# A sorted mixture of experts: third payloads kept by GpSimd at the join, the next first comparison moved between the join's halves, exponentials and joint-point moves reordered

## The reference, cut to what matters

```python
for i in range(E):                                          # 16 experts
    gate_feature = hidden_states * pe[i] @ gate_w + gate_b  # 768 per token
    gate_weight, gate_idx = jax.lax.top_k(gate_feature, K)  # K = 384
    gate_weight = jax.nn.softmax(gate_weight, axis=-1)
    gathered = jnp.take_along_axis(hidden_states, gate_idx, axis=-1)
    y = y + _moe_mlp(gathered * gate_weight, eg_w[i], eu_w[i], ed_w[i])
```

## Time and profile before

| | us |
|---|---|
| median of 3 runs | 6527.94 (6523.31 to 6537.23) |
| profiled execution, its own time | 6528.06 |
| its span in the trace | 6526.2 |
| busy: TensorE, VectorE, ScalarE, GpSimd | 5668.0, 5168.4, 2656.1, 4136.3 |

### The profile page before, as it was taken

One profiled execution on the slowest core, in us unless ns is written; L12 is line 12 of the kernel. 1 busy time (PEld: TensorE's weight loads), 2 busy tenths in 40 slices (PEclk: granted clock), 3 DMA queues, 4 the chain that ended last, 5 costly groups with the idle time before them and its releaser, 6 DMA issues. The chain is left out here.

```text
span 6526.2 us, 70284 instructions
## 1 busy us (share of the span) xinstructions
PE 5668.0 (87%) x16428; PEld 2994.9 (46%) x16428; DVE 5168.4 (79%) x6614; ACT 2656.1 (41%) x4418; POOL 4136.3 (63%) x3675
## 2 busy tenths in 40 slices
PE   8989999889888888888888888888888888889988
PEld 4545554445444444444444444444444444445555
DVE  4011012999999999999999999999999999998841
ACT  0000001445454545454545454555555544544431
POOL 0543034668777777777777777777777776767740
PEclk9999999989999999999999999999999999999999
DMA  3365245000000000000000000000000000001101
GB/s 124 111 158 158 105 143 154 1 22 15 15 15 16 15 16 15 30 1 30 1 30 1 30 14 17 15 16 15 16 16 15 16 15 16 15 30 37 37 25 43
DMA packets 113770, 254.57 MB, mean 39 GB/s; under 512 B 36105, under 2 KB 46863, under 8 KB 113323
## 3 DMA queue, kind: packets, MB, share of 16 engines
q1 hardware_dynamic: 70442, 180.18, 7.9%
q0 software_dynamic: 42880, 69.46, 4.3%
HBM read 214.75 MB, written 34.58 MB: 38 GB/s over the span
## 5 line engine op out<-in xcount | busy, mean ns | idle before, releaser
L1370 PE MATMUL mask_ps<-key,neg_ident 125*125 125x480 f32 (+7 forms) x4128 | 1877.5, 573 | 583.2 <-DVE key L1757 576.9
L1465 POOL TENSOR_TENSOR pay<-pay_side,pay 125x480 int32<-125x480 int32 (+9 forms) x1120 | 1306.7, 1167 | 641.4 <-DVE pay L1780 633.2
L1643 ACT COPY mask_ps<-key 125x960 f32<-125x960 f32 (+7 forms) x1152 | 954.7, 829 | 1706.1 <-DVE pay L1797 1029.0
L1457 POOL TENSOR_TENSOR pay_side<-pay 125x480 int32<-125x480 int32 (+9 forms) x1120 | 1301.2, 1162 | 338.3 <-DVE pay L1797 160.9
L1370 PEld LDWEIGHTS mask_ps<-key,neg_ident 125*125 125x125 f32 x4128 | 729.1, 191 | 1473.6 <-DVE key L1757 1012.8
L1780 DVE COPY_PREDICATED pay<-mask_ps,pay 125x960 f32<-125x960 int32 (+6 forms) x1120 | 1240.4, 1108 | 58.5 <-POOL pay_side L1457 24.0
L1747 DVE TENSOR_TENSOR key<-mask_ps,key 125x960 f32<-125x960 f32 (+6 forms) x1120 | 1091.9, 975 | 61.7 <-PE mask_ps L1370 37.6
L1757 DVE TENSOR_TENSOR key<-mask_ps,key 125x960 f32<-125x960 f32 (+6 forms) x1120 | 1092.7, 976 | 0.0
L1370 PE MATMUL mask_ps<-key_top,neg_ident 125*125 125x480 f32 (+3 forms) x1472 | 607.1, 541 | 139.8 <-DVE key_top L1757 129.3
L1317 PE MATMUL slot_ps<-w_exp,hid 128*125 128x384 f32 x1920 | 672.4, 488 | 8.8 <-issue 8.8
L1289 PE MATMUL slot_ps<-u_feat,w_exp 128*128 128x312 f32 (+1 forms) x2304 | 666.2, 426 | 0.4 <-ACT u_feat L1533 0.4
(11 more groups left out here) (189 smaller groups left out, 5435.9 us busy)
## 6 DMA issues: line engine op xcount, KB each, us to landing
w_rel_g<-L_gnn_W SPq DMA_DIRECT2D x16, 2304.0 KB, 23.4
w_exp<-L_ffn_ed_w SPq DMA_DIRECT2D x16, 2304.0 KB, 8.4
messages_dram<-rows_g SPq DMA_DIRECT2D x12, 1875.0 KB
w_exp<-L_ffn_eg_w SPq DMA_DIRECT2D x16, 1152.0 KB, 5.5
w_exp<-L_ffn_eu_w SPq DMA_DIRECT2D x16, 1152.0 KB, 7.9
messages_dram<-rows_g SPq DMA_DIRECT2D x20, 375.0 KB
root_w_g<-L_gnn_root SPq DMA_DIRECT2D x2, 2304.0 KB
w_exp<-L_ffn_sg_w SPq DMA_DIRECT2D x4, 1152.0 KB, 5.7
```

The source lines that it names most:

```text
L1370: last = pe.matmul(mask, neg_ident[0:TP, 0:TP], operand, start=False, stop=True, skip_group_check=True)
L1457: pool.tensor_tensor(shares(pay_was(turn, u), turn, u)[1].bitcast(I32), first, second, ALU.add).then_inc(pays_added, 1)
L1465: pool.tensor_tensor(second, shares(pay_was(turn, u), turn, u)[1].bitcast(I32), first, ALU.subtract).then_inc(pays_taken, 1)
L1643: act.copy(seed_of(turn, u), compared(turn, u)[0]).then_inc(seeded, 1)
```

## The change

`keep_pays` goes from ScalarE to GpSimd, and from the second half of the join to the first: GpSimd does it at unit 91, after its last shares of units 89 and 90. Keys and payloads kept get a semaphore each. ScalarE seeds the next turn's unit 0 at unit 91, ahead of the payload copies of 91. `preset(2)` moves from unit 0 to unit 1, behind the seed of unit 2. VectorE compares the next turn's unit 0 between the keys of unit 92 and the payloads of 91, not behind the payloads of 91. At joint points VectorE does the second payloads of u-2 ahead of the larger keys of u, not behind. The exponentials go to units 40, 41, 42, 44 and 45, those of 39 to 46 in which ScalarE takes no gate result; the weighing is two units behind each (42, 43, 44, 46, 47), `invert` goes from 46 to 47, the scaling from 47..51 to 48..52, and `BEGIN` stays 52. The early products are spread over units 0 to 51, so that the first part of the first one is in unit 1, not 2, and those behind it in part one unit earlier. The set of free units changes with these, with as many shared columns in it as before (47450).

```diff
-        NSET, NKEPT = 3, 3
+        NSET, NKEPT = 3, 2
...
-        WEIGH = EXPS + 2
-        INVERT = EXPS + NT + 2
+        INVERT = EXPS + NT + 3
         SCALE = INVERT + 1
-        BEGIN = SCALE + NT
+        BEGIN = SCALE + NT - 1
...
-            todo = beside(turn, ahead, lag, 1, BEGIN)
+            todo = beside(turn, ahead, lag, 0, BEGIN)
...
-        REGULAR.free = {u for u in range(REGULAR.n) if not WEIGH <= u < WEIGH + NT
+        gates_taken = {spot - 1 for spot in asking}
+        exps_at = [u for u in range(EXPS, INVERT) if u not in gates_taken][0:NT]
+        weigh_at = [u + 2 for u in exps_at]
+        assert exps_at[NT - 1] < INVERT and weigh_at[0] < SCALE
+        REGULAR.free = {u for u in range(REGULAR.n) if u not in weigh_at
                         and all(work is nothing for work, _ in asking.get(u, []))}
...
+            def keep_pays(turn, i, u):
+
+                pool.wait_ge(pays_done, turn.done("units", i, u))
+                pool.wait_ge(pays_taken, turn.done("sums", i, u))
+                settle(pool, pool_waits)
+                pays = pay[:, :].rearrange("p (i b t) -> p i b t", b=BLK, t=NT)[:, :, 2, :]
+                for half in range(2):
+                    pool.tensor_copy(third_pays[half], pays[:, half * 128:half * 128 + 128, :]).then_inc(kept_pays, 1)
...
-                    if turn is REGULAR and WEIGH <= u < WEIGH + NT:
-                        if u == WEIGH:
+                    if turn is REGULAR and u in weigh_at:
+                        if u == weigh_at[0]:
                             features_sorted(turn, i, SORTED + 1)
-                        weigh(i - 1, u - WEIGH)
+                        weigh(i - 1, weigh_at.index(u))
                     for work, args in todo.get(u, []):
                         work(*args)
+                    if turn.units[u] == (JOIN, 0, 2):
+                        keep_pays(turn, i, u)
...
                     if u + 1 < turn.n:
                         seed(turn, i, u + 1)
-                    elif following is not None:
-                        seed(following, i + 1, 0)
                     if turn is not CLOSING and u == 0:
                         if turn is REGULAR:
-                            act.wait_ge(kept, i * NKEPT)
+                            act.wait_ge(kept_pays, i * NKEPT)
                         preset(0)
                         if turn is REGULAR:
                             act.wait_ge(pays_done, turn.done("units", i, 0))
-                        for q in range(1, NSET):
-                            preset(q)
+                        preset(1)
+                    if turn is not CLOSING and u == 1:
+                        preset(2)
                     if turn.units[u] == (JOIN, 0, 2):
                         keep_keys()
+                        seed(following, i + 1, 0)
                     copy_pays(turn, i, u)
-                    if turn is REGULAR and EXPS <= u < EXPS + NT:
-                        if u == EXPS:
+                    if turn is REGULAR and u in exps_at:
+                        if u == exps_at[0]:
                             keys_sorted(turn, i, i - 1, SORTED + 1)
-                        exponentials(i - 1, u - EXPS)
+                        exponentials(i - 1, exps_at.index(u))
...
-                    if turn.units[u] == (JOIN, 1, 2):
-                        keep_pays()
                     do(todo.get(u, []))
...
                     if turn is REGULAR and u == INVERT:
                         invert(i - 1)
+                    if u in turn.joint:
+                        second_pays(turn, i, u - 2)
                     larger_keys(turn, i, u)
-                    if u > 1:
+                    if u > 1 and u not in turn.joint:
                         second_pays(turn, i, u - 2)
                     smaller_keys(turn, i, u)
...
                 for u in range(max(turn.streams, 1), turn.n):
                     larger_keys(turn, i, u)
                     smaller_keys(turn, i, u)
+                    if turn.units[u] == (JOIN, 1, 2):
+                        larger_keys(following, i + 1, 0)
+                        smaller_keys(following, i + 1, 0)
                     first_pays(turn, i, u - 1)
                     second_pays(turn, i, u - 1)
-                if following is not None:
-                    larger_keys(following, i + 1, 0)
-                    smaller_keys(following, i + 1, 0)
```

More of the change, by code:

```diff
@@ L1064, in experts @@
                                                     sem("mask_made"))
-        kept, bias_set, bias_ready, slots_primed = sem("kept"), sem("bias_set"), sem("bias_ready"), sem("slots_primed")
+        bias_set, bias_ready, slots_primed = sem("bias_set"), sem("bias_ready"), sem("slots_primed")
+        kept_keys, kept_pays = sem("kept_keys"), sem("kept_pays")
         pay_copied, moved, pays_done, pay_set = sem("pay_copied"), sem("moved"), sem("pays_done"), sem("pay_set")
         pays_added, pays_taken = sem("pays_added"), sem("pays_taken")
-        sort_waits = sem("sort_waits")
+        sort_waits, pool_waits = sem("sort_waits"), sem("pool_waits")
         max_ready, exp_ready, inv_ready = sem("max_ready"), sem("exp_ready"), sem("inv_ready")
@@ L1618, in keep_keys @@
             def keep_keys():
-                act.copy(third_key, key[:, :].rearrange("p (i b t) -> p i b t", b=BLK, t=NT)[:, :, 2, :]).then_inc(kept, 1)
-            def keep_pays():
-                pays = pay[:, :].rearrange("p (i b t) -> p i b t", b=BLK, t=NT)[:, :, 2, :]
-                for half in range(2):
-                    act.copy(third_pays[half], pays[:, half * 128:half * 128 + 128, :]).then_inc(kept, 1)
+                act.copy(third_key, key[:, :].rearrange("p (i b t) -> p i b t", b=BLK, t=NT)[:, :, 2, :]).then_inc(kept_keys, 1)
             def preset(q):
@@ L1745, in larger_keys @@
                 if s == FLIP or (s == 0 and turn is not OPENING):
-                    dve.wait_ge(kept, (i - 1) * NKEPT + 1)
+                    dve.wait_ge(kept_keys, i)
                 dve.tensor_tensor(results(turn, u)[0], seed_of(turn, u), compared(turn, u)[1],
@@ L1771, in first_pays @@
                     dve.wait_ge(pays_taken, turn.done("sums", i, turn.needs[u]))
-                    dve.wait_ge(kept, i * NKEPT)
+                    dve.wait_ge(kept_pays, i * NKEPT)
                     settle(dve, sort_waits)
```

## The result

The changed kernel takes 6494.22 us (median of 4 runs, 6481.10 to 6502.65), a ratio to the kernel before of 0.9943 (95% interval 0.9932 to 0.9955): 34 us faster, where 58 were forecast. It is inside the range and nearest to the price of rival A, but not for A's reason. The profiled execution took 6502.65 us, 25.4 less than that of before, though its graph layer, which the change doesn't touch, took 7.5 more.

The account below looks back on a forecast made before the run. VectorE was taken to bound turns 2 to 14. Exponentials 20, joint points 7, join 25 and TensorE's clock 6 gave 58 us off 6528.06: 6470 us, with 6452 to 6502 for 8 in 10.

Parts of the forecast that it names:

- rival A: TensorE's clock and the order of its early products bring an 18 us loss, not the gain: 6494 us; chance 0.08.
- Bound: VectorE bounds turns 2 to 14; only its idle time, at most 10.55 us a turn, can be won.
- Exponentials: VectorE's waits for ScalarE's seeds at units 44 and 45 go: 1.45 us a turn, 20 us in all.
- Joint points: At units 75 and 81 VectorE's second payloads move into its wait for the mask: 0.5 us a turn, 7 us.
- Join: Around unit 92, VectorE's wait for ScalarE's `pay_top` copy goes and unit 0 starts earlier: 1.65 us each, 25 us in all.
- Rival D: GpSimd's copies at the join are slow and `preset(0)` waits; over 8.9 us for both the change loses; chance 0.03.
- the payload copy that the forecast set against it: VectorE's 640-column payload copy took 0.89 us beside GpSimd's `xs` scaling and 0.88 with GpSimd idle.
- Mask of unit 2: Behind the join, an earlier half product fills TensorE's idle time before this mask: 0.5 us a turn, 6 us.

Follow-up runs that it names:

- e7: The changed kernel with the two copies of the third payloads on ScalarE again, all else as changed: 6500.49 us, ratio 0.9962 to the kernel before.
- e5: The kernel before with only the order of moves at the joint points changed: 6526.3 us, ratio 0.9994 to the kernel before.
- e12: The changed kernel with early products and free units as before, but TensorE does the first product's first half in unit 1, not 2: 6482.85 us, ratio 0.9929.
- e2: The changed kernel with its free units computed from the old spread of early products: 6481.5 us, ratio 0.9929 to the kernel before; run again 6484.78 us, 0.9926.
- e1: The changed kernel with early products spread from unit 1 as before, so also the old column shares in the first 37 units: 6484.86 us, ratio 0.9941.
- e10: The changed kernel with the old free units, plus an unused half product on TensorE behind the masks of units 6, 76 and 84: 6478.49 us, ratio 0.9925.

## Why the prediction was right in its direction and short in its size

**Bound.** Right: VectorE's idle time was what could be won, and 7 us of 10 are still there.

**Exponentials** (forecast 1.45 us a turn). The seed waits went from 1.59 to 0.28, and from the larger keys of unit 43 to those of 50 a turn has 23.3 us in place of 25.0. Right.

**Joint points** (0.5). 0.4 at the place. Right, and too small to be seen alone.

**Join** (1.65). 1.3 to 1.7, 1.68 in the turn shown, with the residual wait of 0.46 on the preset named beforehand. Right. GpSimd's copies took 0.79 and 0.80 us, which is the lower bound, not the 2.5 us for both that I took. Rival D falls, and e7 shows that the copies needn't have moved. VectorE's comparisons beside them took 1.16 us each (2026.94), as in e7, where GpSimd stood idle. The lock of which the Trainium skill's page "SBUF — State Buffer", section "Who interferes with whom", tells needs two SBUF inputs for a `tensor_tensor` on VectorE; these comparisons have one (the seed lies in PSUM), so their agreement says nothing against it. Nor does the payload copy that the forecast set against it: its mask lies in PSUM, and beside that it takes one input from SBUF.

**Mask of unit 2** (0.5). 0.63 to 0.66 in 12 turns and 0.47 in one. The idle time ahead of this mask fell from 3.12 to 1.80 us; it takes 1.88 us in 8 of 13 turns and 2.3 to 3.0 in the others, and VectorE waits for it in one turn only, 0.09 us. Right in its size; that TensorE would work nearly without a break was not so, and e5 shows that this wait goes in some turns without the early product. The 18 us of rival A didn't come. The new wait before L1782 did (0.49 a turn), and e12 shows that some 0.3 of it count.

**The step that failed** is a sentence: "VectorE's and GpSimd's shares stay, since the free units hold the same number of columns". They do hold the same number (47450), but I counted the columns of the free units and not what freeing does in each. In units with two rows it does nothing, so VectorE's columns rose from 28835 to 29555 a turn. It costs 1.0 us a turn, 13 us, and e2 shows it by undoing it: its shortest turns take 313.2 us, and "about 313" was forecast.

**What the forecast did not have** is the clock's answer. I multiplied one turn's gain by 13. The kernel before is undisturbed in 12 of 13 turns; the changed one loses 11 to 19 us in 5 to 7 disturbed turns (the 13 turns less 13 times the shortest: 22.1 and 13.5, before 2.9). 13 for the shares and the lower of these, 11, are the 24 us that are missing; with the higher it would be 32, and single executions differ by that much, so the two account for the gap only roughly. This also makes the parts not add up: alone they are worth 8, 2 and 0 us, 10 together, where e1, which has all three and the products of before, gains 38 us (0.9941, 0.9928 to 0.9955).

Open: what sets the turn in which the clock falls. The runs show that it changes when the timing of a turn is changed and from one execution to the next, that some turns recur, and that filling one gap is answered by falls at another; no run predicts a place. Whether a turn length near 317.2 us is a good one by itself, or whether before's order happened to fit it, was not separated either. The shortest turns of e2, e10 and e12 all take 313.2 us, and 4 to 10 of their turns are disturbed, so length alone doesn't decide it.

## What to carry to other kernels

A gain per iteration is only worth its multiple if the iterations stay alike: where TensorE has idle gaps of some 2 us ahead of work that another engine waits for, compare iterations with each other by their steps, not only one with one, and expect a small part tested alone to read as nothing. When a rule picks the units that get a larger share, sum what each engine really gets under it, unit by unit, not the units that it names. And before work is moved to another engine to make room, look whether the queue that it leaves had room once the other moves are made.

## What was not expected of the hardware

Behind the same idle time of 2.03 to 2.04 us the same mask was made in 1.59 us (granted clock 1.00) or in 2.29 to 3.00 us (0.77 to 0.50), by when the turn came. 1.67 us of work added to VectorE in each turn changed the time by nothing (1.0001 against 0.9998). A GpSimd copy of 640 columns with one input took 0.79 us, as long as on ScalarE (0.79) and half of GpSimd's difference with two inputs.
